# A fused perceiver block on one core: three ACT copies change places in the queue with the gate's exponent

## What is computed

```
x = x + attention(layernorm(x), context of 257 rows a sequence, LoRA on q, k, v, o)
# the time-mix block, on z = layernorm(x)
xn = ln(z, g1, b1);  xx = xn shifted by one token
k, v = mix(xn, xx) @ Wk, mix(xn, xx) @ Wv;   r = sigmoid(mix(xn, xx) @ Wr)
wkv = scan over the 32 tokens (exponentially decayed sums of exp(k) * v and exp(k))
x = x + z + (r * wkv) @ Wo
logits = ln(...) @ router_w;  softmax; top 2 of 8 experts, two weights a token
x = x + sum over the 2 experts of sigmoid(xr @ eWr) * (relu(xk @ eWk)^2 @ eWv)
# the last block, on layernorm(x): a shared GEGLU and the best one of 8 GEGLU experts
x = x + geglu(xf, w1s, w2s, w3s) + geglu(xf, W1[e], W2[e], W3[e])
```

## Time and profile before

| | |
|---|---|
| median of 3 runs | 939.2 us (938.8 to 939.45) |
| the profiled execution: its own time, its span | 936.4 us, 934.7 us |
| granted PE clock on the mean | 0.967 of 2.4 GHz |
| busy: PE, DVE, ACT, POOL | 855.4, 431.3, 337.2, 343.3 us |
| busy from 103 to 145 us, of 42: PE, DVE, ACT, POOL | 37.33, 36.76, 29.23, 28.89 us |

### The profile page before, as it was taken

One profiled execution on the slowest core, in us unless ns is written; L12 is line 12 of the kernel. 1 busy time (PEld: TensorE's weight loads), 2 busy tenths in 40 slices (PEclk: granted clock), 3 DMA queues, 4 the chain that ended last, 5 costly groups with the idle time before them and its releaser, 6 DMA issues.

```text
span 934.7 us, 18917 instructions
## 1 busy us (share of the span) xinstructions
PE 855.4 (92%) x6360; PEld 768.8 (82%) x6360; DVE 431.3 (46%) x1316; ACT 337.2 (36%) x753; POOL 343.3 (37%) x580
## 2 busy tenths in 40 slices
PE   5899988887568989999959999999999999999998
PEld 4567767665467879999948999999999999999998
DVE  1269988889883544444324766521111111111114
ACT  1366776675464546665521111111111111111110
POOL 1444677775877445554213332020011000000033
PEclk8899999999779989999988999999999999999999
DMA  9875457335422322262212111157889988997114
GB/s 352 268 262 207 168 176 244 113 135 209 131 80 64 81 58 85 81 220 83 67 51 63 58 57 58 63 198 265 314 296 319 325 322 309 309 317 280 57 52 135
DMA packets 92110, 162.00 MB, mean 173 GB/s; under 512 B 13832, under 2 KB 71112, under 8 KB 88680
## 3 DMA queue, kind: packets, MB, share of 16 engines
q1 hardware_dynamic: 71008, 103.39, 32.8%
q10 hardware_dynamic: 12832, 37.82, 10.9%
q0 software_dynamic: 8176, 19.57, 8.0%
HBM read 146.10 MB, written 14.66 MB: 172 GB/s over the span
## 4 chain that ended last, share of the span: by engine, by line
PE 69%; DVE 10%; POOL 7%; issue 5%; DVEq 5%; DMA 3%; ACT 1%; ACTq 1%; SPq 0%; POOLq 0%
PE bank L1642 27%; PE bank L1655 14%; PE bank L372 7%; PE bank L399 7%; PE bank L386 3%; DMA xz<-in_x_dram 2%; PE bank L361 2%; PE bank L774 1%; POOL tab_e L680 1%; PE bank L783 1%; DVEq L1388 1%; DVE arena_b L1186 1%; PE bank L799 1%; PE bank L839 1%; PE bank L861 1%
## 5 line engine op out<-in xcount | busy, mean ns | idle before, releaser
L1642 PEld LDWEIGHTS bank<-arena_b,arena_a 128*128 128x128 f32 x1472 | 168.0, 192 | 1.2
L1642 PE MATMUL bank<-arena_b,arena_a 128*128 128x128 f32 x1472 | 168.1, 275 | 0.0
L1708 ACT ACTIVATE arena_b<-bank 128x512 f32<-128x512 f32 x78 | 46.6, 597 | 300.5 <-PE bank L1642 300.5
L1850 DVE TENSOR_TENSOR arena_b<-bank,arena_b 128x512 f32<-128x512 f32 x78 | 53.9, 692 | 191.9 <-PE bank L1642 188.5
L1642 PE MATMUL bank<-arena_b,a_x 128*128 128x128 f32 x1024 | 122.7, 280 | 0.0
L1642 PEld LDWEIGHTS bank<-arena_b,a_x 128*128 128x128 f32 x1024 | 119.8, 196 | 0.4
L328 POOL DMA_INDIRECT arena_a<-rows_e,pick x78 | 76.1, 975 | 28.9 <-issue 28.3
L1655 PE MATMUL bank<-arena_a,arena_b 128*128 128x256 f32 x368 | 83.2, 379 | 0.0
L372 PE MATMUL bank<-arena_b,arena_a 128*128 128x128 f32 x624 | 80.2, 284 | 0.5 <-DVE arena_b L503 0.5
L1546 POOL COPY pick<-list_i 128x1 uint32 x23 | 4.2, 184 | 206.6 <-PE bank L1625 180.5
L372 PEld LDWEIGHTS bank<-arena_b,arena_a 128*128 128x128 f32 x624 | 76.9, 201 | 0.9 <-DVE arena_b L503 0.8
(11 more groups left out here) (275 smaller groups left out, 1354.5 us busy)
## 6 DMA issues: line engine op xcount, KB each, us to landing
arena_a<-in_W_dram SPq DMA_DIRECT2D x69, 1024.0 KB, 7.6
arena_a<-in_ctx_n_dram ACTq DMA_DIRECT2D x16, 1152.0 KB, 6.9
arena_a<-in_ctx_t_dram SPq DMA_DIRECT2D x16, 1028.0 KB, 6.4
rows_y<-arena_a ACTq DMA_DIRECT2D x39, 128.0 KB, 1.7
arena_a<-in_w_moe_dram ACTq DMA_DIRECT2D x3, 1156.0 KB, 5.4
arena_a<-in_w_moe_dram ACTq DMA_DIRECT2D x3, 1152.0 KB, 7.6
rows_f<-arena_b ACTq DMA_DIRECT2D x23, 128.0 KB, 6.2
rows_e<-arena_b SPq DMA_DIRECT2D x64, 32.0 KB, 3.8
```

What stands on the lines that cost most here:

```text
L1642: last = nc.tensor.matmul(bank[half][:, f * P:(f + 1) * P], w12[:, i, k, col0:col0 + P], zT[:, k], start=k == 0, stop=k == KD - 1)
L1708: nc.scalar.activation(act_g[:, half], bU[half][:], ACT.Gelu).then_inc(g_ac_g, 1)
L1850: nc.vector.tensor_tensor(hT_f[:, u % 2, half * HH:(half + 1) * HH].rearrange("p f t -> p (f t)"), bG[half][:], act_g[:, half], ALU.mult). ...
```

## The change

ACT's loop calls the same stages in another order. In steps below MOE_AT the logits copy and the time-mix input copy stand behind `gate_exp` and `hidden`; from MOE_AT on the order is as it was. No instruction, wait or buffer is added or removed. After the edit the lines behind it have numbers that are 2 higher in the loop and beyond.

```diff
                 if c is not None:
                     normed1(c)
-                if live(s - LAG + 1) is not None:
-                    copy_in(s - LAG + 1)
                 if k is not None:
                     gate_exp(k)
                 if live(s + 1) is not None:
                     hidden(s + 1)
+                if g is not None and s < MOE_AT:
+                    router(g)
+                if live(s - LAG + 1) is not None:
+                    copy_in(s - LAG + 1)
                 if s >= MOE_AT:
                     moe(s - MOE_AT)
-                if g is not None:
+                if g is not None and s >= MOE_AT:
                     router(g)
                 if a is not None:
                     softmax(a)
```

## The result

| | before | changed |
|---|---|---|
| median, runs of the first comparison | 939.0 us (938.75 to 939.45, 4 runs) | 932.97 us (929.53 to 934.55, 4 runs) |
| profiled execution: its own time, its span | 936.4, 934.7 us | 929.53, 927.8 us |
| L1246 (L1248 after) that ended the wait of 1.99 us, start | 242.56 us | 234.40 us |

The medians differ by 6.0 us, where 6.3 were forecast. The ratio of the runs is 0.9927, 95% interval 0.9908 to 0.9946, which is 6.9 us of 939.0. In two later sets of rounds, on chips 12 and 7, the changed kernel stood at 0.9919 (0.9894 to 0.9945) and 0.9915 (0.9895 to 0.9936), 7.6 and 8.0 us. All three intervals hold the forecast, and all three middles lie above it. Of the kernel before, three executions of the first later set (1264, 1266 and 3025 us) were disturbed and are in no ratio and no median here.

The account below looks back on a forecast made before the run. The prediction took DVE, standing at L1246 for logits queued behind ACT's wait for L640, as the bound. Waits removed, 6.9 us, less 0.6 added gave 6.3 gained: 932.9 us from the 936.4 profiled plus 2.8 to the median; range 930.8 to 936.9.

Parts of the forecast that it names:

- the wait of 1.99 us: DVE's largest wait for the logits, ending at L1246 at 242.56 us; forecast to go whole.
- The place in the queue, not work: ACT's L1024 waits 1.20 us for L640, holding four instructions that don't need it; moving L1024 behind them recovers the time.
- a wait for PE under another name: Rival, chance 0.06: PE's results come 0.5 us later than read, DVE waits for PE through ACT; about 939 us.
- PE's L754 doesn't set the pace: Denies the slower rival, chance 0.05: L754 paces, later L1010 costs 0.42 us in each of 13 steps; 944.7 us.
- 6.9 us of waits removed: At DVE's L1246: 7.7 us of waits for the logits, less two that stay, 0.43 and 0.41.
- a margin of 0.06 us: At the step of 242.56, logits let DVE go at 240.51, DVE arrives at 240.57, so the wait just goes whole.
- DVE's own step, 13.42 us: L1246 to L1246 without the wait: 14.19 us less 0.77, which becomes the bound.
- meetings of DVE and GpSimd: Rival, chance 0.10: DVE's L1231 and POOL's L654 slow each other, costing 3.9 and 1.0 us; 937.8 us.
- 0.6 us lost in the early steps: Later L1010 delays PE's L754 by 0.28 us in step 5, repeated in step 6; bounds 0 and 2.1 us.
- POOL's loop of 12.6 us behind DVE's: POOL's loop through L658, L974 and L1246, next in line as bound, 0.8 us below DVE's 13.42.
- Given back at the entrance of the experts: Rival, chance 0.15: after 242.56 DVE waits for POOL's two gathers, losing 1.99 us plus 1.34 of clock; 936.2 us.
- The sum: Whole kernel: 6.9 less 0.6 gives 6.3 us gained, median 932.9 us; chance 0.64.

Follow-up runs that it names:

- rstd1_first: Kernel before with one GpSimd edit: rstd1 (ending in L640) ahead of rstd3, ACT's order unchanged; 931.03 us against 936.42 before, ratio 0.9944.
- router_behind: Changed kernel with the logits copy moved back behind the time-mix input copy; 934.71 us against 939.69 for the kernel before, ratio 0.9959.
- gate_only: Kernel before with L1024 moved behind the gate only, still ahead of L980 and L1075; 931.63 us against 936.42 before, ratio 0.9946.
- swap_after_2: Second measurement of the changed kernel with DVE's running maximum ahead of the one-hot; 932.16 us against 939.6 for the kernel before, ratio 0.9914.
- both_edits: Changed kernel with the old order in steps below 7 and DVE's running maximum ahead of the one-hot; 926.21 us (936.42 before), later 929.92 (939.6 before).
- three_edits: both_edits plus GpSimd's rstd1 ahead of rstd3; 932.73 us against 939.6 for the kernel before, ratio 0.9917.
- again: The changed kernel, unedited, measured and profiled once more; 932.32 us against 939.69 for the kernel before, ratio 0.9919.
- changed_2: The changed kernel, unedited, measured in the third set; 931.63 us against 939.6 for the kernel before, ratio 0.9915.

## Why the prediction was right, and where two of its sizes were off

- **The place in the queue, not work.** Right. Busy times hardly moved (DVE 433.4 us, ACT 334.7), DVE's wait for L1075 fell to 1.6 us against about 1.5 forecast, and rstd1_first removed the waits of the middle steps from the other end. That it didn't become a wait for PE under another name, and that PE's L754 doesn't set the pace, is in the same rows: DVE has no wait in the middle steps, and PE still has 4.0 us of waits for it at L839.
- **6.9 us of waits removed.** Right, the 1.99 whole too, in spite of a margin of 0.06 us. router_behind and gate_only show what it hangs on: with L1024 ahead of the logits again, its wait for L640 (0.70) and its own 0.4 brought back about 1.1 us of it.
- **DVE's own step, 13.42 us.** The term that was mis-sized: it measured 12.95. The step was taken as the old one less its wait, with the durations unchanged. But the wait had set where GpSimd's L658 fell, on top of the one-hot, and with the wait the overlap went. The prediction priced meetings of DVE and GpSimd as a loss only, on other lines; here they became fewer, there as well (the longest L1231, L1233 after, takes 426 ns now, 903 before). Over the stretch DVE's step is 2.0 us more gain than forecast, of which the one-hot is 1.1.
- **0.6 us lost in the early steps.** Right in kind and place, half the size: 0.28. Counted from the first L783 of the table, PE's L754 came 0.23, 0.10 and 0.26 us later in the three steps from 68 us on, so the two delays of 0.28 didn't add up.
- **POOL's loop of 12.6 us behind DVE's.** Not contradicted: DVE's step fell to 12.95 us, and to 12.92 in swap_after_2, with no wait in its place. No run went down to 12.6, so the loop's size isn't shown.
- **Given back at the entrance of the experts.** It wasn't. The lead of 8.16 us at 242.56 was still 7.66 at the last L1246 (292.36 before, 284.70 after) and 7.70 at the first such row of the last block (L1754, 490.65 before, 482.95 after). The window of the earlier trace rows holds later work in the changed kernel, so its equal clock, 0.80, says little; over the 50 us behind the stretch it is 0.80 before and 0.76 after. The window's row:

```profile
243.00:293.00 50.00, 35.35 (x199) 31.01 (x200) 30.33 (x99) 23.01 (x47) 38.74 (x60) 0.80 0.28 81
```

- **The sum.** 8.16 us were ahead at 242.56, and 6.9 at the end of the span. The forecast of 6.3 stands against 6.0 by the medians of the first comparison, and 7.4 and 8.0 later. That the first came within 0.3 was partly luck: the two errors of size, 2.0 and 0.3, both made the gain larger than forecast, and what varies behind the stretch took about as much back.

What varies there is the last section's subject. It is larger than either error, and a prediction to a microsecond could not have had it.

## What to carry to other kernels

Where an engine's queue is in a fixed order, look for an instruction that waits for a late producer with others behind it that don't need that producer. Such a wait costs only what the next engine stands still for, and it can be removed by moving the waiter back or by hurrying its producer. When a wait goes, don't keep the other durations fixed: look at what DVE and GpSimd were doing relative to each other during it. And before the kernel is compared at the median, compare one stretch of it behind the first loads and ahead of what varies, since here a stretch repeated to 0.03 us where medians of six runs moved by one or two. Then take the stretch step by step: the gain of an edit should stand in the steps that it touches and in no other.

## What was not expected of the hardware

**A small DVE instruction took three times as long beside a GpSimd one.** The one-hot (128x16, two inputs in SBUF) takes 0.17 us alone and 0.54 when L658 (128x256, 0.84 us) is under way, and ends just after it; with the running maximum ahead of it, it took 0.15 to 0.17 in all middle steps. The Trainium skill (SBUF — State Buffer, Who interferes with whom) says that a DVE instruction with two SBUF inputs contends with a GpSimd instruction that reads SBUF, and calls such contention an exclusive lock. The traces agree: the one-hot's end in the step of the earlier trace rows is 147.37, L658's 147.34. The running maximum L1192, which takes its place beside L658, has one of its inputs in PSUM and takes 0.69 us there, against 0.68 before.

**ACT stood still with no cause in the records.** In the changed kernel, ACT's rows around the experts' entrance:

```profile
274.36 0.60 ACT L430 ACTIVATE h_relu<-bank 128x512 f32<-128x512 f32 x1 [3.00 <-remote]
...
292.18 0.60 ACT L430 ACTIVATE h_relu<-bank 128x512 f32<-128x512 f32 x1 [3.91 <-remote]
292.87 0.63 ACT L433 ACTIVATE hT<-h_relu 128x512 f32<-128x512 f32 x1
...
296.58 0.38 ACT L423 ACTIVATE arena_b<-bank 128x256 f32<-128x256 f32 x1 [1.88 <-remote]
```

PE's 16 matmuls, the only thing that L430 waits for, had ended 3.9 us before its start at 292.18. The kernel before has no such time in its profile. The nine profiles of kernels with the new order in the first comparison and the first and third sets all have it, 9 to 13 us of idle time; the four of the second set, both_edits among them, have none. Their rests average 695.1 and 691.3 us, 3.8 us apart; how much of that is the idle time isn't shown, since the kernels and chips differ too. It looks like something of the chip or session and not of the change: both_edits ran 3.7 us slower in the third set than in the second, and the kernel before 3.2. The profiled execution of the kernel before, 936.4 us and without it, fits its median of 936.42 in the second set, while its medians in the others are 939.0 to 939.7, which would fit if they hold it. No profile of the kernel before in a set that has it was taken, so this stays open, and with it how much of the 6 to 8 us it hides or lends. A smaller one, 0.76 to 4.44 us, stands at 129 to 132 us ahead of L980 or L1069 in nine of the fourteen profiles, among them gate_only and rstd1_first, which are edits of the kernel before; the longest, in three_edits:

```profile
131.09 0.47 ACT L1069 ACTIVATE arena_b<-bank,r_low 128x256 f32<-128x256 f32 x1 [4.44 <-remote]
```

It takes back part of what was gained before it. The packets of the two instruction queues in the trace were compared with these times and don't line up with them. What ACT waits for was not found.

**The clock.** Behind 220 us PE's granted clock falls to the lower level of 1.2 GHz in some stretches, and how much of it there is differs between executions of one kernel: over the 50 us behind the stretch the mean was 0.81 in again and 0.74 in changed_2. That is 3.5 us of full clock, but it isn't 3.5 us of time: again, with the higher clock, has the longer rest, 696.9 against 694.8. In the second set gate_only had 0.71 there and rstd1_first 0.83, 6 us of full clock apart, and their rests are 691.8 and 690.5. So the mean clock of a part in which PE often waits is no price by itself. Whether the slow groups stood on the chain in one execution and not in the other was not looked at.
